# A graph network kernel: edge terms in two buffers, bias transfers inside the loop, and three groups of node rows loaded in the block before

## The chip, the cores and the metric

The kernel runs on one core of a Trainium2 chip. The metric is the device time of one execution in microseconds; the time before and after is the median of several runs. The kernel is written directly in Bass: each engine has its own instruction stream, and all ordering between engines is by semaphores that the author has placed.

## The reference, cut to what matters

```python
h = relu(layernorm(x))                                   # x: 50000 nodes x 128
x = x + leaky(( h + scatter(h[src]*ew/sqrt(deg..)) ) @ W0.T + b0)      # 12500 edges
h = relu(layernorm(x))
for l in range(4):                                       # graph attention, self loops added
    hw = h @ W[l]
    a  = leaky((hw @ a_s)[src] + (hw @ a_d)[dst] + (ea @ We[l]) @ a_e, 0.2)
    a  = segment_softmax(a, dst)
    h  = layernorm(segment_sum(hw[src] * a, dst) + b[l]) * g[l] + beta[l]
x = x + h
```

Most nodes have no edge. For those a layer is a fixed map of the node's own row, so all layers are done in one pass over the row ("dense"). Only the rows that edges touch go through the layers one at a time. `ea @ We[l]` meets only a fixed vector, so an edge needs just four numbers from its attributes, one for each layer: its edge terms.

## The kernel before, in words

The 50000 rows are 100 groups of 500 (125 partitions x 4 rows of 128 floats). The program is a chain of blocks; a block ends when all five engines have come to its end, and nothing of the next block starts earlier.

1. **Setup** (first block): weights, bias products, the scan columns of the edges. It ends with the four folded bias rows in `END[0:4]` (called `E4`).
2. **The setup loop** (second block, `with nc.Block()` after L636): 25 steps of 500 edges. SP loads the source numbers (L796) and target numbers (L177, L178 through `dma2`) of each step as a row that is broadcast to all partitions. DVE makes the masks and counts; PE turns the edge attributes and multiplies them by `VE` (L738) to a 4 x 500 tile of edge terms in PSUM; DVE copies that tile to the SBUF buffer `AES` (`keep_edge_term`, L683), and SP stores it to `term_t` (`place_edge_term`, L789). There is one `AES`: the copy of step g waits until the store of step g-1 has landed (`s_aet`). After the last step SP moves the bias rows of `E4` to the block matrix `EB`, 16 transfers of one row each (L813, L815), and waits for them. GpSimd (POOL) meanwhile gathers the first `SOON` = 44 of the 100 columns of source rows (L222); each gather is one indirect DMA of 125 rows, and it waits for nothing.
3. **The first dense block**: 36 groups. POOL runs the remaining gathers beside it, again without a wait.
4. **`conv_layer`**: the first layer of the touched rows.
5. Four times **a dense block of 16 groups and `attention(l)`**. In the dense block POOL gathers the rows of `row_t` that the preceding block has stored; it waits first for all those stores (`s_x1`, `s_rows`), then runs its 100 gathers, and the block cannot end before they have landed.

A dense block keeps 12 groups in a ring `X` in SBUF. At its start SP issues the loads of the first 12 groups, two DMAs each (112 and 13 partitions), and DVE's first `bn_stats` (L1051) waits for the first of them. The ring shares its memory with the masks `M` of `conv_layer` and `attention`: slots 0 to 2 lie where the mask of the first pairs lies. At the end of `conv_layer` and `attention` a side chain (END, XTX, a row of T) runs after the last pair of columns, step by step through PE, DVE and ACT, and SP stores its result last (L1348 and L1350, or L1823).

`wait_stores` makes SP wait at the start of such a block until all output rows of the dense block are written, before the masks are loaded over the ring.

Of the kernel before, what the change touches and what calls it, by code (L numbers as in the profile page):

```python
# [11 lines left out]
D = 128  # L12
N = 50000
E = 12500
L = 4
P = 125
C = E // P
# [14 lines left out]
SOON = 44  # L32


def gnn_kernel(nc, x, src, dst, ea, ew, w0, b0, wg, we, att_s, att_d, att_e, bg, gamma, beta, out):
    ctx = ExitStack()
    with ctx:
# [5 lines left out]
        def sem(name):  # L43
            return ctx.enter_context(nc.semaphore(name))
# [231 lines left out]
        VT = RB[0:C, 6700:6700 + D]  # L276
# [337 lines left out]
        s_aet = sem("edge_term_transposed")  # L614
# [19 lines left out]
        AES = AL[0:L, :, :].rearrange("l a e -> l (a e)")  # L634
        with nc.Block() as block:
# [7 lines left out]
            def _(dve):  # L643
# [35 lines left out]
                def keep_edge_term(g):  # L679
                    dve.wait_ge(s_aep, g + 1)  # L680
                    if g:
                        dve.wait_ge(s_aet, 16 * g)
                    nc.vector.tensor_copy(AES, PT[2 + g % 2][0:L, 0:Q * P]).then_inc(s_aes, 1)  # L683

# [93 lines left out]
            def _(sp):  # L778
                src_v = src_t.rearrange("t e -> (t e)")
                dst_v = dst_t.rearrange("t e -> (t e)")  # L780

                def keep_masks(k):
                    sp.wait_ge(s_mask, (k + 1) * EG // 5)
                    c0, c1 = k * C // 5, (k + 1) * C // 5
                    dma2(sp, m_v[:, c0:c1, :], M[:, c0:c1, :], s_mst)

                def place_edge_term(g):
                    sp.wait_ge(s_aes, g + 1)
                    sp.dma_start(term_t[:, g * Q * P:(g + 1) * Q * P], AES).then_inc(s_aet, 16)  # L789

                for g in range(EG):
                    if g >= 7:
                        place_edge_term(g - 7)
                    if g >= 3:
                        sp.wait_ge(s_ge, g - 2)
                    sp.dma_start(SRCB[g % 3], src_v[g * Q * P:(g + 1) * Q * P].unsqueeze(0)  # L796
                                 .broadcast_to([C, Q * P])).then_inc(src_rows[g % 3].s, 16)
                    if g >= 4:
                        sp.wait_ge(s_mask, g - 3)
                    dma2(sp, TGTB[g % 4], dst_v[g * Q * P:(g + 1) * Q * P].unsqueeze(0).broadcast_to([P, Q * P]),  # L800
                         dst_rows[g % 4].s)
                    if g > 5 and g % 5 == 3:
                        keep_masks(g // 5 - 1)
# [5 lines left out]
                sp.wait_ge(s_e4, 1)  # L809
                sp.wait_ge(s_ebz, 1)  # L810
                for a in range(Q):
                    for j in range(3):
                        sp.dma_start(EB[j * Q + a:j * Q + a + 1, a * D:(a + 1) * D],  # L813
                                     E4[j + 1:j + 2, :]).then_inc(s_eb, 16)
                    sp.dma_start(EB[KS - 1:KS, a * D:(a + 1) * D], E4[0:1, :]).then_inc(s_eb, 16)  # L815
                sp.wait_ge(s_eb, 16 * 4 * Q)
                sp.wait_ge(s_aet, 16 * EG)
# [10 lines left out]
        def dense(first_group, groups, moves, move, arrive, early=None):  # L828
# [39 lines left out]
            with nc.Block() as block:  # L868
# [11 lines left out]
                def _(sp):  # L880
                    for g in range(min(XS, groups)):
                        dma2(sp, rows(g), x_v[first_group + g], loaded[g % XS].s)
# [417 lines left out]

        def wait_stores(sp):
            for s in range(XS):
                sp.wait_ge(*signal(f"ring_stored_{s}").at(0))
# [16 lines left out]
        def conv_layer():  # L1320
# [13 lines left out]
            with nc.Block() as block:  # L1334
                @block.sync
                def _(sp):
                    wait_stores(sp)
                    load_masks(sp)
                    sp.dma_start(AE[:, :, :], term_t.rearrange("l (t e) -> t l e", t=C)).then_inc(s_aet, 16)
# [6 lines left out]
                    sp.wait_ge(s_aet, 16 * EG + 16)  # L1346
# [356 lines left out]
        def attention(l):  # L1703
# [100 lines left out]
            with nc.Block() as block:  # L1804
                @block.sync
                def _(sp):
# [10 lines left out]
                    else:  # L1817
                        for i in range(STORES):
                            c0, c1 = 2 * i * STORE, 2 * (i + 1) * STORE
                            sp.wait_ge(*t_ready.at((i + 1) * STORE))  # L1820
                            dma2(sp, row_v[:, c0:c1, :], T[:, c0:c1, :], s_rows)
                        sp.wait_ge(*x_act.at(1))
# [227 lines left out]
        for l in range(L):  # L2050
            targets = Targets(l)
            dense(done, SHARES[l + 1], C, refresh(l), [(s_refresh, 16 * C * (l + 1))], targets)
# [26 lines left out]
```

## Time and profile before

| | us |
|---|---|
| median of 3 runs | 2042.78 |
| the three runs | 2036.03, 2042.78, 2043.71 |
| the profiled execution | 2044.88 |
| its span in the trace | 2042.8 |
| mean granted clock of TensorE | 0.878 of full |

| stage | about from | to |
|---|---|---|
| setup | 0 | 48.7 |
| setup loop | 48.7 | 164.6 |
| dense, 36 groups | 164.6 | 510 |
| `conv_layer` | 510 | 763.7 |
| dense 0, attention 0 | 763.7 | 1064.8 |
| dense 1, attention 1 | 1064.8 | 1369.4 |
| dense 2, attention 2 | 1369.4 | 1673.9 |
| dense 3, attention 3 (final) | 1673.9 | 2042.8 |

A row of the timeline gives start, duration, engine, line, operation and, in brackets, the idle time ahead of it with what ended it. "SPq" rows are the moments at which SP issues a DMA, not the transfer itself. A row with "x3" merges several instructions.

### The profile page before, as it was taken

Reading aid. Unit: us, or ns where it says so; the run is one execution under the profiler, and the core shown is the slowest. Engines: PE = TensorE matmul, PEld = TensorE weight load, DVE = VectorE, ACT = ScalarE, POOL = GpSimd, SP = SyncE. Lnnn points to the kernel's source line nnn. Section 1 sums busy time; section 2 is a strip of 40 time slices with the busy share of each in tenths; the row PEclk is TensorE's granted clock in tenths of the full one; section 3 lists DMA queues with packets and bytes.
Section 4 is the critical chain, followed back from the end, with each engine's and each line's share of the span. In section 5 each row is a group of like instructions: output and inputs, shape, how many; then the busy total and the mean of one; then the engine's idle time right before and its main releaser. Section 6 shows DMA issues by size and latency. Waiting matters only on the chain. (4 is left out here: it accounts for less than half of the span.)

```text
span 2042.8 us, 40093 instructions
## 1 busy us (share of the span) xinstructions
PE 1536.4 (75%) x9041; PEld 1123.4 (55%) x9041; DVE 1630.1 (80%) x8491; ACT 1545.9 (76%) x7842; POOL 1089.7 (53%) x919
## 2 busy tenths in 40 slices
PE   3764888886788877885978884978875978875940
PEld 2433555553677764544975544975544975543830
DVE  5775999996899967986877986877986877986940
ACT  0674999996799967993987983988983978973730
POOL 0876787750455538772008771018771018772777
PEclk9996999998799977995997996988996988996975
DMA  8753233321321122213231213231213231214421
GB/s 165 194 145 91 73 100 97 97 72 37 92 67 55 55 71 65 60 41 85 66 101 39 61 45 79 68 109 33 61 41 90 67 107 25 61 45 119 110 53 34
DMA packets 134375, 157.14 MB, mean 77 GB/s; under 512 B 58714, under 2 KB 91879, under 8 KB 134137
## 3 DMA queue, kind: packets, MB, share of 16 engines
q1 hardware_dynamic: 77545, 128.36, 22.6%
q0 software_dynamic: 56160, 25.44, 6.0%
q8 instruction: 74, 1.21, 0.2%
q14 instruction: 164, 1.34, 0.2%
q10 hardware_dynamic: 432, 0.79, 0.1%
HBM read 106.25 MB, written 68.36 MB: 85 GB/s over the span
## 5 line engine op out<-in xcount | busy, mean ns | idle before, releaser
L222 POOL DMA_INDIRECT S<-row_t,rowI x400 | 537.9, 1345 | 562.0 <-DMA row_t<-T 422.4
L938 PE MATMUL bank<-AC,XT 128*125 128x390 f32 x800 | 327.9, 516 | 0.3
L1007 ACT ACTIVATE R<-bank 125x128 f32<-125x128 f32 x1200 | 322.8, 306 | 0.0
L1007 ACT ACTIVATION_READ_ACCUMULATOR R<-bank 125x1 f32 x1200 | 279.7, 240 | 0.0
L210 PE MATMUL bank<-ident,Y 125*128 125x125 f32 x800 | 131.2, 290 | 118.0 <-ACT Y L958 59.2
L1870 PE MATMUL bank<-WCX,XT 128*125 128x130 f32 (+1 forms) x1400 | 218.7, 279 | 0.1
L210 PEld LDWEIGHTS bank<-ident,Y 125*128 125x128 f32 x800 | 97.9, 150 | 218.3 <-issue 140.7
L222 POOL DMA_INDIRECT S<-in_x,srcI x100 | 157.9, 1579 | 99.7 <-issue 99.7
L1051 DVE BATCH_NORM_STATS2 st<-R 125x6 f32<-125x128 f32 x800 | 173.2, 279 | 31.0 <-issue 30.6
L1870 PEld LDWEIGHTS bank<-WCX,XT 128*125 128x125 f32 x1400 | 182.6, 189 | 6.7 <-ACT XT L1907 0.4
L918 PEld LDWEIGHTS bank<-AC,XT 128*125 128x125 f32 x800 | 105.6, 204 | 114.2 <-ACT SB L1024 112.6
L918 PE MATMUL bank<-AC,XT 128*125 128x128 f32 x800 | 124.7, 303 | 56.2 <-ACT SB L1024 55.0
L222 POOL DMA_INDIRECT T<-in_x,dstI x101 | 142.2, 1408 | 36.9 <-issue 36.9
L1849 PE MATMUL bank<-R,S 125*128 125x125 f32 x800 | 159.0, 281 | 2.9 <-DVE R L1955 1.9
L226 POOL DMA_INDIRECT out_rows<-T,repNI x101 | 123.4, 1221 | 70.6 <-DVE T L2012 39.4
L938 PEld LDWEIGHTS bank<-AC,XT 128*125 128x125 f32 x800 | 133.7, 197 | 44.5 <-ACT XT L991 8.6
L1851 PE MATMUL bank<-R,T 125*128 125x125 f32 x800 | 158.0, 280 | 0.0
L1029 ACT ACTIVATE R<-bank 125x128 f32<-125x128 f32 x400 | 108.5, 321 | 40.0 <-PE bank L922 39.1
L217 PE MATMUL bank<-W,R 128*125 128x128 f32 x800 | 128.8, 310 | 0.0
L1849 PEld LDWEIGHTS bank<-R,S 125*128 125x128 f32 x800 | 124.5, 196 | 3.6 <-DVE R L1955 2.1
L1897 ACT ACTIVATE R<-ident,aselfS 125x125 f32<-125x125 f32 x300 | 107.8, 431 | 23.2 <-PEq L1710 23.2
L1851 PEld LDWEIGHTS bank<-R,T 125*128 125x128 f32 x800 | 124.8, 197 | 0.0
(447 smaller groups left out, 4755.1 us busy)
## 6 DMA issues: line engine op xcount, KB each, us to landing
row_t<-T SPq DMA_DIRECT2D x40, 573.1 KB
R<-in_x SPq DMA_DIRECT2D x100, 224.0 KB
out_rows<-R SPq DMA_DIRECT2D x100, 224.0 KB
R<-m_t SPq DMA_DIRECT2D x25, 546.9 KB
S<-row_t,rowI POOLq DMA_INDIRECT x400
T<-in_edge_attr SPq DMA_DIRECT2D x5, 1120.0 KB
x_t<-XB SPq DMA_DIRECT2D x50, 112.0 KB
R<-x_t SPq DMA_DIRECT2D x25, 224.0 KB
```

What stands on the lines that cost most here:

```text
L210: ins = nc.tensor.transpose(ps[:, a * P:(a + 1) * P], t, ident[0:P, 0:P])
L217: ins = nc.tensor.matmul(pz[0:P, a, :], xt[:, a * P:(a + 1) * P], w, start=False, stop=True, skip_group_check=True)
L222: pool.indirect_dma_start(to, None, table, bass.IndirectOffsetOnAxis(ap=idx, axis=0), bounds_check=rows - 1, oob_is_err=False).then_inc(do ...
L226: pool.indirect_dma_start(table, bass.IndirectOffsetOnAxis(ap=idx, axis=0), frm, None, bounds_check=rows - 1, oob_is_err=False).then_inc(d ...
L918: nc.tensor.matmul(last_of(g)[:, a, :], h0(g, a), AC[3], start=a == 0, stop=False, skip_group_check=True)
L938: nc.tensor.matmul(LAYERS[a][0:P, 0:3 * D + 6], h0(g, a), ACB[:, 0:3 * D + 6], start=True, stop=True).then_inc(layers_done.s, 1)
L1007: ins = nc.scalar.activation(JUNK[:, a * 3 + l, :], LAYERS[a][0:P, l * D:(l + 1) * D], ACT.Square, scale=D ** -0.5, accum_out=NRM[:, g % N ...
L1029: ins = nc.scalar.activation(JUNK[:, 12 + a, :], last_of(g)[:, a, :], ACT.Square, scale=D ** -0.5, accum_out=ss4[:, g % NS, a:a + 1])
L1051: ins = nc.vector.bn_stats(ring[:, a, :], v[:, a, :])
L1849: nc.tensor.matmul(o, S[:, 2 * n + a, 0:D], MA[:, r, a, :], start=True, stop=False, skip_group_check=True)
L1851: ins = nc.tensor.matmul(o, T[:, 2 * n + a, 0:D], DGB[:, r, a, :], start=False, stop=True, skip_group_check=True)
L1870: ins = nc.tensor.matmul(product(banks[bank + r], 2 * P)[:, a, :], XT[:, r, xt + a * P:xt + (a + 1) * P], WCX[:, l, 0:cols], start=not fin ...
```

## The change

Three edits, and constants that go with them.

- **Edge terms in two buffers.** `AES` becomes a list of two: the old place in `AL` for even steps and columns 6300 to 6800 of `R` for odd ones. `s_aet` becomes two semaphores. The copy of step g now waits for the store of step g-2. The table `VT`, whose place the new buffer takes, moves to column 10900.
- **Bias transfers in the loop.** The 16 transfers of `E4` to `EB` leave the end of the block and go, one per step, into steps 2 to 17 of SP's loop (`place_bias`), behind the loads of that step.
- **`SOON` from 44 to 38.** POOL does 38 gathers in the setup loop and 62 of this kind in the first dense block.
- **Loads ahead.** The loads of groups 0 to 2 of each of the four dense blocks of 16 groups are issued by SP near the end of the block before (`load_ahead`), behind a wait that the last mask has been used (`masked.at(NU)`) and before the store of the side chain's result. The dense block's own load loop starts with group 3. The first dense block is left as it was.

```diff
-SOON = 44
+AHEAD = 3
+SOON = 38
...
-        VT = RB[0:C, 6700:6700 + D]
+        VT = RB[0:C, 10900:10900 + D]
...
-        s_aet = sem("edge_term_transposed")
+        s_aet = [sem("edge_term_placed_even"), sem("edge_term_placed_odd")]
...
-        AES = AL[0:L, :, :].rearrange("l a e -> l (a e)")
+        AES = [AL[0:L, :, :].rearrange("l a e -> l (a e)"), RB[0:L, 6300:6300 + Q * P]]
...
                 def keep_edge_term(g):
                     dve.wait_ge(s_aep, g + 1)
-                    if g:
-                        dve.wait_ge(s_aet, 16 * g)
-                    nc.vector.tensor_copy(AES, PT[2 + g % 2][0:L, 0:Q * P]).then_inc(s_aes, 1)
+                    if g >= 2:
+                        dve.wait_ge(s_aet[g % 2], 16 * (g // 2))
+                    nc.vector.tensor_copy(AES[g % 2], PT[2 + g % 2][0:L, 0:Q * P]).then_inc(s_aes, 1)
...
+                def place_bias(a, j):
+                    if a == 0 and j == 0:
+                        sp.wait_ge(s_e4, 1)
+                        sp.wait_ge(s_ebz, 1)
+                    k = j * Q + a if j < 3 else KS - 1
+                    sp.dma_start(EB[k:k + 1, a * D:(a + 1) * D], E4[(j + 1) % L:(j + 1) % L + 1, :]).then_inc(s_eb, 16)
...
                     dma2(sp, TGTB[g % 4], dst_v[g * Q * P:(g + 1) * Q * P].unsqueeze(0).broadcast_to([P, Q * P]),
                          dst_rows[g % 4].s)
+                    if 2 <= g < 18:
+                        place_bias((g - 2) // Q, (g - 2) % Q)
...
-                sp.wait_ge(s_e4, 1)
-                sp.wait_ge(s_ebz, 1)
-                for a in range(Q):
-                    for j in range(3):
-                        sp.dma_start(EB[j * Q + a:j * Q + a + 1, a * D:(a + 1) * D],
-                                     E4[j + 1:j + 2, :]).then_inc(s_eb, 16)
-                    sp.dma_start(EB[KS - 1:KS, a * D:(a + 1) * D], E4[0:1, :]).then_inc(s_eb, 16)
...
-                    for g in range(min(XS, groups)):
+                    for g in range(loaded_before, min(XS, groups)):
                         dma2(sp, rows(g), x_v[first_group + g], loaded[g % XS].s)
...
+        def load_ahead(sp, first_group):
+            for g in range(AHEAD):
+                dma2(sp, X[:, g * Q:(g + 1) * Q, :], x_v[first_group + g], signal(f"ring_loaded_{g}").s)
...
+                        sp.wait_ge(*masked.at(NU))
+                        load_ahead(sp, sum(SHARES[0:l + 2]))
                         sp.wait_ge(*x_act.at(1))
                         sp.dma_start(row_v[0:C, C, :], T[0:C, C, :]).then_inc(s_x1, 16)
```

SP's stream at the end of the setup loop, before (`EB<-END` is a bias transfer, `term_t<-AL` the store of an edge term, `R<-in_x` the next block's first load):

```order
L789 DMA term_t<-AL 4x500 x4
L177 DMA m_t<-R 112x2500
L178 DMA m_t<-R 13x2500
L789 DMA term_t<-AL 4x500 x3
L813 DMA EB<-END 1x16x8 x3
L815 DMA EB<-END 1x16x8
```

The same place now:

```order
L797 DMA term_t<-R 4x500
L178 DMA m_t<-R 112x2500
L179 DMA m_t<-R 13x2500
L797 DMA term_t<-AL 4x500
L797 DMA term_t<-R 4x500
L797 DMA term_t<-AL 4x500
L636 UNCONDITIONAL_BRANCH
```

The 16 transfers that stood behind the last edge term are gone from the end; each now stands behind the target loads of one step, and the stores alternate between the two buffers.

SP's stream at the end of attention 0, before (`row_t<-T 100x131` is the store of the side chain's result):

```order
L177 DMA row_t<-T 112x1310
L178 DMA row_t<-T 13x1310
L1823 DMA row_t<-T 100x131
L1804 UNCONDITIONAL_BRANCH
L879 UNCONDITIONAL_BRANCH
L177 DMA R<-in_x 112x512
L178 DMA R<-in_x 13x512
```

The same place now:

```order
L178 DMA row_t<-T 112x1310
L179 DMA row_t<-T 13x1310
L178 DMA R<-in_x 112x512
L179 DMA R<-in_x 13x512
L178 DMA R<-in_x 112x512
L179 DMA R<-in_x 13x512
L178 DMA R<-in_x 112x512
L179 DMA R<-in_x 13x512
L1835 DMA row_t<-T 100x131
L1814 UNCONDITIONAL_BRANCH
L883 UNCONDITIONAL_BRANCH
```

Six load issues now stand between the last large row store and the small one. At the end of `conv_layer` they stand before the two stores of the side chain in the same way.

## Rows read from the trace of the kernel before

**Rows 1.** The page, busy time of each engine (share of the span) and instructions.
```profile
PE 1536.4 (75%) x9041; PEld 1123.4 (55%) x9041; DVE 1630.1 (80%) x8491; ACT 1545.9 (76%) x7842; POOL 1089.7 (53%) x919
```

**Rows 2.** Busy time of each engine from 150 to 200 us, then clock, DMA share, GB/s.
```profile
150.00:200.00 50.00, 20.65 (x80) 13.35 (x80) 27.65 (x167) 21.45 (x94) 28.12 (x22) 0.63 0.36 89
```

**Rows 3.** Timeline of SP's DMA issues at the end of the setup loop.
```profile
150.50 2.39 SPq L789 DMA_DIRECT2D term_t<-AL  x2
153.00 1.85 SPq L813 DMA_DIRECT2D EB<-END  x3
...
164.63 0.34 SPq L177 DMA_DIRECT2D R<-in_x  x1
```

**Rows 4.** The group of DVE's edge-term copies, and the last one in the timeline.
```profile
L683 DVE COPY AL<-bank 4x500 f32<-4x500 f32 x25 | 16.6, 663 | 18.8 <-DMA term_t<-AL 18.8
...
151.95 0.67 DVE L683 COPY AL<-bank 4x500 f32<-4x500 f32 x1 [1.48 <-DMA term_t<-AL]
```

**Rows 5.** Waits of SP's queue: total us, times, longest.
```profile
SPq L789 <- DVE AL L683: 40.4, 22, 3.2
```

**Rows 6.** Busy time in two stretches of the loop, as in rows 2.
```profile
56.00:66.00 10.00, 9.61 (x46) 5.93 (x44) 8.16 (x18) 7.42 (x24) 8.31 (x6) 1.00 0.84 195
...
106.00:116.00 10.00, 6.29 (x40) 4.10 (x40) 7.08 (x16) 8.51 (x33) 8.78 (x5) 1.00 0.75 203
```

**Rows 7.** Timeline of POOL: the first, the 38th and the 44th gather of the loop.
```profile
49.69 1.43 POOL L222 DMA_INDIRECT S<-in_x,srcI  x1 [46.11 <-issue]
...
132.22 1.27 POOL L222 DMA_INDIRECT S<-in_x,srcI  x1 [0.30 <-issue]
...
146.51 1.27 POOL L222 DMA_INDIRECT S<-in_x,srcI  x1 [0.30 <-issue]
```

**Rows 8.** The page's group of `bn_stats`, and timelines at the heads of dense blocks.
```profile
L1051 DVE BATCH_NORM_STATS2 st<-R 125x6 f32<-125x128 f32 x800 | 173.2, 279 | 31.0 <-issue 30.6
...
167.64 0.29 DVE L1051 BATCH_NORM_STATS2 st<-R 125x6 f32<-125x128 f32 x1 [15.02 <-issue]
...
763.71 0.32 SPq L177 DMA_DIRECT2D R<-in_x  x1
...
766.60 0.29 DVE L1051 BATCH_NORM_STATS2 st<-R 125x6 f32<-125x128 f32 x1 [3.65 <-issue]
...
1064.78 0.32 SPq L177 DMA_DIRECT2D R<-in_x  x1
...
1064.79 1.28 ACT L973 ACT_TABLE_LOAD   x1 [0.80 <-PEq L1804]
...
1067.51 0.29 DVE L1051 BATCH_NORM_STATS2 st<-R 125x6 f32<-125x128 f32 x1 [3.96 <-issue]
```

**Rows 9.** End of attention 0: DMA traffic in one microsecond, the side store, POOL's first gather.
```profile
1062.00:1063.00 1.00, 0.59 (x4) 0.37 (x3) 0.26 (x1) 0.00 (x0) 0.00 (x0) 1.00 0.98 299
...
1064.02 0.27 SPq L1823 DMA_DIRECT2D row_t<-T  x1
...
1066.50 1.27 POOL L222 DMA_INDIRECT S<-row_t,rowI  x1 [130.59 <-DMA row_t<-T]
```

**Rows 10.** Last gather and DVE's last work of dense 0 and 3; POOL's last of all.
```profile
934.58 1.33 POOL L222 DMA_INDIRECT S<-row_t,rowI  x1 [0.30 <-issue]
...
938.86 0.69 DVE L1207 TENSOR_TENSOR R<-R 125x512 f32<-125x512 f32 x1
...
1843.59 1.58 POOL L222 DMA_INDIRECT S<-row_t,rowI  x1 [0.30 <-issue]
...
1849.76 0.69 DVE L1207 TENSOR_TENSOR R<-R 125x512 f32<-125x512 f32 x1
...
2037.96 1.19 POOL L226 DMA_INDIRECT out_rows<-T,repNI  x1 [0.30 <-issue]
```

**Rows 11.** SP's slowest DMA issue, in the first block.
```profile
35.01 5.78 SPq L178 DMA_DIRECT2D T<-in_edge_attr  x1
```

More of the change, by code:

```diff
@@ L788, in place_edge_term @@
                     sp.wait_ge(s_aes, g + 1)
-                    sp.dma_start(term_t[:, g * Q * P:(g + 1) * Q * P], AES).then_inc(s_aet, 16)
+                    sp.dma_start(term_t[:, g * Q * P:(g + 1) * Q * P], AES[g % 2]).then_inc(s_aet[g % 2], 16)
                 for g in range(EG):
@@ L808, in _ @@
                     place_edge_term(g)
-                sp.wait_ge(s_e4, 1)
-                sp.wait_ge(s_ebz, 1)
-                for a in range(Q):
-                    for j in range(3):
-                        sp.dma_start(EB[j * Q + a:j * Q + a + 1, a * D:(a + 1) * D],
-                                     E4[j + 1:j + 2, :]).then_inc(s_eb, 16)
-                    sp.dma_start(EB[KS - 1:KS, a * D:(a + 1) * D], E4[0:1, :]).then_inc(s_eb, 16)
                 sp.wait_ge(s_eb, 16 * 4 * Q)
-                sp.wait_ge(s_aet, 16 * EG)
+                sp.wait_ge(s_aet[0], 16 * (EG - EG // 2))
+                sp.wait_ge(s_aet[1], 16 * (EG // 2))
                 sp.wait_ge(s_mst, 160)
@@ L826, in gnn_kernel, with dense @@
             k.base += 32
-        def dense(first_group, groups, moves, move, arrive, early=None):
+        def dense(first_group, groups, moves, move, arrive, early=None, loaded_before=0):
             loaded = [signal(f"ring_loaded_{s}") for s in range(XS)]
@@ L1338, in _ @@
                     load_masks(sp)
-                    sp.dma_start(AE[:, :, :], term_t.rearrange("l (t e) -> t l e", t=C)).then_inc(s_aet, 16)
+                    sp.dma_start(AE[:, :, :], term_t.rearrange("l (t e) -> t l e", t=C)).then_inc(s_aet[0], 16)
                     for n in range(NU):
@@ L1345, in _ @@
                             dma2(sp, row_v[:, 2 * (n + 1 - STORE):2 * n + 2, :], T[:, 2 * (n + 1 - STORE):2 * n + 2, :], s_rows)
-                    sp.wait_ge(s_aet, 16 * EG + 16)
+                    sp.wait_ge(s_aet[0], 16 * (EG - EG // 2) + 16)
+                    sp.wait_ge(*masked.at(NU))
+                    load_ahead(sp, SHARES[0])
                     sp.wait_ge(*x_stage.at(10))
@@ L1821, in _ @@
                             dma2(sp, row_v[:, c0:c1, :], T[:, c0:c1, :], s_rows)
+                        sp.wait_ge(*masked.at(NU))
+                        load_ahead(sp, sum(SHARES[0:l + 2]))
                         sp.wait_ge(*x_act.at(1))
@@ L2051, in gnn_kernel @@
             targets = Targets(l)
-            dense(done, SHARES[l + 1], C, refresh(l), [(s_refresh, 16 * C * (l + 1))], targets)
+            dense(done, SHARES[l + 1], C, refresh(l), [(s_refresh, 16 * C * (l + 1))], targets, AHEAD)
             targets.end()
```

## The prediction, made before the changed kernel was run

> **What bounds the kernel now.** I read the page first. DVE is busy for 80% of the span and ACT for 76% [rows 1]; no engine is full over the whole, so the time that can be won lies in stages where both are idle together. The table of stages shows such a stretch between 150 and 200 us, where PE has 20.65, DVE 27.65 and ACT 21.45 us of work in 50 [rows 2]. The timelines around it say why. DVE's last edge-term copy starts at 151.95 [rows 4], the last store of terms is issued by 152.9, and then SP issues one bias transfer after another from 153.00 on; the next block's first load is issued only at 164.63 [rows 3]. All engines stand at the block's end for that time, and SP alone sets it.
>
> Inside the loop DVE is nearly the bound, but it idles 18.8 us in front of its 25 copies, all of it until a term store has landed [rows 4]. That is a ring: copy, issue, landing, next copy.
>
> Third, the heads of the dense blocks. The group of `bn_stats` has 31.0 us of idle time before it, 30.6 of it "issue" [rows 8], and five waits make it up: 15.02 at the first dense block (which includes the bias tail), 3.65 and 3.96 at the next two, so 8.0 for the last two together, 4.0 each. In the second of these SP issues the load at 1064.78 and DVE starts at 1067.51; ACT, which needs no load, starts at 1064.79.
>
> **The bias transfers.** From the last term store to the next block is now 152.65 (the second of the two issues at 150.50; the merged row ends at 152.89) to 164.63, 12.0 us. Without the 16 transfers SP waits only for that store. The store issued at 150.50 released the copy at 151.95, so landing takes 1.45 us, and a change of block takes 0.5 (SP's 1064.02 + 0.27 to 1064.78 in rows 8 and 9). That leaves 2.0 us: **10.0 us gained**. The price in the loop: one transfer per step, at up to 0.62 us of SP (1.85 for three), 10 us in all. SP waits 40.4 us in the loop for the copies alone [rows 5], so this fits. Behind each stands the next term store and the next loads, which are asked for two to three steps ahead; the waits for `E4` and the cleared `EB` were met one block earlier and cost nothing.
>
> **Two buffers.** The 18.8 us of DVE's idle time can go at most, since a store then has two steps to land. What comes next is DVE itself or the DMA engines. The 25 steps run from about 56 to 152.6, 3.9 us each; 18.8 / 25 = 0.75 of it is this idle time, so DVE's own floor is about 3.1. They are busy for 0.75 of the time at 203 GB/s in one stretch and 0.84 at 195 in another [rows 6]. The loop's bytes stay the same while it shrinks by a fifth, so the share must rise from about 0.7 towards 0.85, and landings get slower behind the mask stores. I take 15.6 of the 18.8, about a sixth off for that. Ends: 18.8 if nothing else comes late, 0 if the loop is held by its transfers anyway. The idle time of DVE names landings only and never a source or target row, so I choose near the upper end.
>
> The Trainium skill, in "DMA: Bandwidth & Descriptors", section "Why a DMA increments its semaphore by 16 and not by 1", says that a transfer of 100 partitions is spread over 10 of the 16 DMA engines only. The source rows have 100 partitions. By that rule the mean share of 0.75 hides ten fuller engines, and the loop would gain perhaps half as much; no view here splits the share by engine, so it only adds to the chance of the second rival.
>
> **`SOON`.** POOL's 38th gather starts at 132.22 and ends at 133.5, the 44th ends at 147.8 [rows 7]. The loop should now end near 152.65 - 15.6 = 137.1, plus 2.0 for landing and block: the next block starts at about 139. With 44 gathers POOL would have held the block until 148; with 38 it has some 5 us to spare. The six gathers that move run in the first dense block, beside ACT and DVE at work; six times the gather's 1.6 us there is 10 us, and POOL's stream in that block ends long before the block does. I cost it at nothing; if that cover were gone it would be those 10 us.
>
> **Loads ahead.** DVE could start about 0.1 us after SP's first issue in the block: 766.60 - 763.81 = 2.8 us, 1067.51 - 1064.88 = 2.6, and the last two like the second (idle 4.0 against 3.96), 10.7 together. ACT's table load of 1.28 us [rows 8] ends at 1066.07; ACT needs it after DVE's statistics, 1.3 us after the new start, 1066.2, so it just stays hidden.
>
> Two things can take some of it back. First, the six load issues, 2.4 us of SP, stand before the side store. At attention 0 the last large row store has been issued by 1061.3 and the side store goes at 1064.02 [rows 9], so they fit with 0.3 us to spare. But their 750 KB stand before the small store in the DMA engines: at 299 GB/s [rows 9] 2.5 us of traffic, of which about 1.7 is still ahead of it. POOL's first gather, now at 1066.50, may start up to 1.7 us later. The first group itself stands behind 640 KB of rows; that traffic is over at about 1063.4 and 250 KB take 0.84 us, so it lands just in time. At `conv_layer` SP has no work between 754.5 and 760.8 and nothing is delayed.
>
> Second, POOL's 100 gathers may end a dense block last. In dense 0 the last gather ends at 935.91 and DVE at 939.55, SP's stores 0.8 later; in dense 3 it is 1845.17 and 1850.45 [rows 10]. DVE moves up by 2.8 and 2.65, POOL does not, or goes back by 1.7 in dense 3. What is left, with the 0.8, is 1.6 and 1.7 us for the last gather to land. That landing isn't shown alone: from POOL's last instruction at 2039.15 to the span's end at 2042.8 are 3.65 us, which bounds it from above, and the edge-term store's 1.45 is the nearest row below. I take 1.7, between them and near the lower one because the upper holds the end of the program too. So dense 0 and 3 sit at the edge; at 3.65 each would lose 2 us. In dense 1 and 2 POOL's last gather ends over 7 us before DVE, and nothing is lost. I take off 1.0 in all: **9.7 us gained**, with 6 and 10.7 as ends.
>
> **The sum.** 10.0 + 15.6 + 9.7 = 35.3 us. Against the profiled execution, 2044.88 (span 2042.8, 2.1 outside it), that is 2009.6. The median of the runs is 2.1 lower, 2042.78, which gives 2007.5; I say **2008**. A measurement tells about 0.5%, 10 us, from no change.
>
> **Rivals.**
>
> *DMA holds the loop* (0.13). The share goes to its limit and the landings move back with it. For it: 0.84 at only 195 GB/s in rows 6. Against: other stretches move 299 GB/s. Then the two buffers bring 0 to 8 of the 15.6: 2015 to 2023.
>
> *POOL ends the setup loop last* (0.10). Its gathers take 2.23 us each on average here, against 1.6 alone. If they slow down in proportion to the DMA share, 0.7 to 0.84, it is 2.7 each, and 38 of them end at 152: 13 us are lost, 2021. For it: gathers in the loop are already slow. Against: they are delayed by a fixed number of bytes, which doesn't grow. The Trainium skill, "DMA: Bandwidth & Descriptors", section "Queues, rings and completion order", has each DMA engine take turns between the queues it has work for, packet by packet. By that a denser SP queue costs each gather more; it is what this rival would rest on.
>
> *The heads give little* (0.09). POOL's chain, not DVE's, ends the dense blocks, or the first group isn't there: 2 to 5 us instead of 9.7, 2012 to 2016.
>
> *The change does not do what it says* (0.04), because the block's end is held by something that no row names: within 5 us of before, 2040.
>
> *Slower* (0.02). SP issues can stall: one took 5.78 us behind five large loads [rows 11]. If each of the six loads ahead took over about 2.5 us, the side store would be 13 us late in four blocks, of which 2 to 5 are slack: 4 x 9 = 36 us, which eats the whole gain; at the full 5.78 it is 2090. It decides at 2.5 us per issue; the same loads now take 0.4.
>
> **How the numbers follow.** The forecast itself has 0.62. Its own range, from the ends of the parts, is 2000 (18.8 and 10.7 in full, and a run as low as the fastest of before) to 2014. To hold 8 in 10 I reach to most of the next two rivals: 1999 to 2020. Faster by over 0.5%: 0.94; the same 0.04; slower 0.02.
>
> **What would show it.** In the changed kernel's trace: SP's first load of the first dense block at 139, not before 136 nor after 146; DVE's copies with under 4 us of idle time; no bias transfers behind the last term store; POOL's 38th gather over by 137; the idle time of `bn_stats` down from 30.6 to about 9 us, with heads of about 1.2; POOL's first gather in dense 1 to 3 up to 1.7 us further behind the block's start; the last landing and DVE's end within 1 us of each other in dense 0 and 3. If the copies' idle time is gone but source, target or gather rows show new waits, the rival on DMA is right; if the heads shrink and the dense blocks' lengths from their start grow by as much, POOL's chain ended them.

## The result

The changed kernel takes **2013.8 us** (median of four runs, 2012.8 to 2016.1) against 2041.8 for the kernel before: a ratio of 0.9869, 95% interval 0.9847 to 0.9891. The forecast was 2008 with a range of 1999 to 2020. The profiled execution has a span of 2010.8 us, 32.0 less than before. All that follows about places is read from it. In the changed code L683 has become L684, L789 L797, L177 and L178 L178 and L179, L222 L223, L1051 L1055 and L1823 L1835.

```profile
PE 1526.6 (76%) x9041; PEld 1114.3 (55%) x9041; DVE 1629.9 (81%) x8491; ACT 1546.6 (77%) x7842; POOL 1089.0 (54%) x919
...
L1055 DVE BATCH_NORM_STATS2 st<-R 125x6 f32<-125x128 f32 x800 | 172.9, 277 | 16.1 <-issue 8.9
```

The busy times are those of [rows 1] within 10 us; what went is idle time. That before `bn_stats` fell from 31.0 [rows 8] to 16.1.

Where it went shows when one lists SP's first load of each block that starts with loads. The convolution's length is in the second line.

| block starts at | before | after | gained so far | gained in the stage |
|---|---|---|---|---|
| first dense block | 164.63 | 140.09 | 24.5 | setup 24.5 |
| dense 0, behind the convolution | 763.71 | 734.80 | 28.9 | 4.4 |
| dense 1 | 1064.78 | 1034.77 | 30.0 | 1.1 |
| dense 2 | 1369.36 | 1337.93 | 31.4 | 1.4 |
| dense 3 | 1673.88 | 1641.35 | 32.5 | 1.1 |
| end of the span | 2042.8 | 2010.8 | 32.0 | -0.5 |

The setup gave 24.5 where 25.6 was forecast, the heads of dense 0 to 3 gave 3.1 instead of 9.7, and 4.4 came in a stage to which the forecast gave nothing. Within the setup the two terms came out otherwise than forecast: the last copy ends 18.2 us earlier (152.62 to 134.44) where 15.6 was forecast, and from there to the next block it is 5.65 us instead of 12.0, a gain of 6.4 where 10.0 was forecast.

**The end of the setup loop.** First the groups of DVE's copies by shape, which answer [rows 4], then SP's waits in the loop, as [rows 5], then the timelines of SP and POOL, which answer [rows 3] and [rows 7]:

```profile
L684 DVE COPY AL<-bank 4x500 f32<-4x500 f32 x13 | 8.6, 659 | 1.3 <-DMA term_t<-AL 1.2
L684 DVE COPY R<-bank 4x500 f32<-4x500 f32 x12 | 7.9, 659 | 2.4 <-DMA term_t<-R 2.4
```
```profile
SPq L797 <- DVE R L684: 9.9, 6, 3.4
SPq L797 <- DVE AL L684: 6.9, 8, 2.6
SPq L636 <- PEq L636: 3.7, 1, 3.7
```
```profile
133.88 0.24 SPq L797 DMA_DIRECT2D term_t<-R  x1
134.46 0.24 SPq L797 DMA_DIRECT2D term_t<-AL  x1
140.09 0.33 SPq L178 DMA_DIRECT2D R<-in_x  x1
```
```profile
133.23 1.27 POOL L223 DMA_INDIRECT S<-in_x,srcI  x1 [0.30 <-issue]
134.81 1.27 POOL L223 DMA_INDIRECT S<-in_x,srcI  x1 [0.30 <-issue]
140.95 1.27 POOL L223 DMA_INDIRECT S<-in_x,srcI  x1 [4.87 <-issue]
```

DVE idles 3.7 us before its copies instead of 18.8, and no bias transfer stands behind the last term store. But that store's issue starts at 134.46 and the next block comes 5.6 us later, where the forecast had 2.0; SP stands 3.7 us of it at the block's end with its own work done. The last thing running is POOL's 38th gather, which ends at 136.08, 4.0 us before the block. The windows show the hole (busy time of PE, PEld, DVE, ACT and POOL, then clock, DMA share and GB/s, as in [rows 2]): everything but POOL has next to nothing to do there.

```profile
125.00:135.00 10.00, 6.43 (x35) 3.35 (x33) 9.01 (x18) 7.76 (x29) 8.48 (x6) 0.98 0.33 94
135.00:145.00 10.00, 0.00 (x0) 0.00 (x0) 1.26 (x11) 0.30 (x1) 4.52 (x4) 0.50 0.42 108
```

**A head.** The timeline at the start of dense 1, answering [rows 8] and [rows 9]:

```profile
1032.77 0.31 ACT L1951 ACTIVATE YX<-T 100x128 f32<-100x128 f32 x1 [2.46 <-DVE T L2041]
1032.98 0.19 ACT L1951 ACTIVATION_READ_ACCUMULATOR YX<-T 100x1 f32 x1
...
1033.49 0.39 SPq L179 DMA_DIRECT2D R<-in_x  x1
1033.93 0.33 SPq L1835 DMA_DIRECT2D row_t<-T  x1
1034.77 0.32 SPq L178 DMA_DIRECT2D R<-in_x  x1
...
1034.86 0.29 DVE L1055 BATCH_NORM_STATS2 st<-R 125x6 f32<-125x128 f32 x1 [2.12 <-PEq L1814]
...
1037.91 1.27 POOL L223 DMA_INDIRECT S<-row_t,rowI  x1 [133.18 <-DMA row_t<-T]
```

DVE starts 0.1 us behind SP, as forecast (0.1 at dense 0 and 2 too, 0.5 at dense 3); before it was 2.7. But the side store (L1835) waits for the last of the six load issues: ACT is done at 1033.17 and the store goes at 1033.93, 0.76 us later. And POOL's first gather comes 3.14 us behind the block's start; it was 1.72.

**An end.** The timeline at the end of dense 2. `m_t` is the next block's first load, normally issued 1.7 us behind the end of the last output store:

```profile
1509.78 1.27 POOL L223 DMA_INDIRECT S<-row_t,rowI  x1 [0.30 <-issue]
...
1511.56 0.32 SPq L178 DMA_DIRECT2D out_rows<-R  x1
1511.92 0.39 SPq L179 DMA_DIRECT2D out_rows<-R  x1
...
1515.11 0.32 SPq L178 DMA_DIRECT2D R<-m_t  x1
```

Here it comes 2.8 us behind that store and 4.1 us behind the last gather's end (1511.05). Dense 3 is alike, 3.3 and 4.5 us. Against the usual 1.7 that is 1.1 and 1.6 us lost.

### The profile page after: what moved, and what is told of

The parts are those of the page before. It is cut to its first block and busy times, and to the rows that moved or that the text cites. A ratio compares the mean times of both kernels' runs of the same rounds, so it can differ in the third digit from the quotient of the medians.

```text
span 2010.8 us, 40093 instructions
## 1 busy us (share of the span) xinstructions
PE 1526.6 (76%) x9041; PEld 1114.3 (55%) x9041; DVE 1629.9 (81%) x8491; ACT 1546.6 (77%) x7842; POOL 1089.0 (54%) x919
## 5 line engine op out<-in xcount | busy, mean ns | idle before, releaser
L223 POOL DMA_INDIRECT S<-row_t,rowI x400 | 537.8, 1344 | 560.8 <-DMA row_t<-T 420.7
L223 POOL DMA_INDIRECT S<-in_x,srcI x100 | 158.3, 1583 | 83.6 <-issue 83.6
L1055 DVE BATCH_NORM_STATS2 st<-R 125x6 f32<-125x128 f32 x800 | 172.9, 277 | 16.1 <-issue 8.9
L227 POOL DMA_INDIRECT out_rows<-T,repNI x101 | 124.2, 1230 | 68.0 <-issue 34.7
L223 POOL DMA_INDIRECT T<-in_x,dstI x101 | 140.4, 1390 | 37.4 <-issue 37.4
```

The lines of the kernel that those rows point to most:

```text
L223: pool.indirect_dma_start(to, None, table, bass.IndirectOffsetOnAxis(ap=idx, axis=0), bounds_check=rows - 1, oob_is_err=False).then_inc(do ...
L227: pool.indirect_dma_start(table, bass.IndirectOffsetOnAxis(ap=idx, axis=0), frm, None, bounds_check=rows - 1, oob_is_err=False).then_inc(d ...
L1055: ins = nc.vector.bn_stats(ring[:, a, :], v[:, a, :])
```

## The experiments

Three questions were open: what holds the end of the setup loop, where the heads' gain went, and whether the 4.4 us belong to the change. Places are read from the profile of each run, and all differences in a total are taken from its ratio to the kernel before.

**1. Fewer and more gathers in the setup loop.**

```diff
-SOON = 38
+SOON = 30
```


> The changed kernel with SOON at 30 instead of 38: eight gathers fewer in the setup loop, eight more in the first dense block. In the changed kernel the last term store is issued at 134.5 and POOL's 38th gather ends at 136.1, but the next block's first load comes only at 140.1. Theory (POOL holds the block, about 3.5 us behind its last gather): POOL is through long before, the block ends by SP's last landing, and the first load of the first dense block comes at 134.7 + 1.45 + 0.5 = 136.7; 3.4 us are gained there. Rival 1 (the last term store lands late, after about 4.9 us): the first load stays at 140. Rival 2 (POOL's eight gathers more lengthen the first dense block): the first load comes at 136.7, but the block's length from there grows by up to 8 x 1.6 = 13 us. Total by the theory 2010, by rival 1 2014, by rival 2 up to 2023.

```diff
-SOON = 38
+SOON = 44
```


> The changed kernel with SOON at 44, as in the kernel before. Six gathers more in the setup loop, at 1.6 us alone: the last one starts near 134.8 + 9.5 = 144.3 and ends at 145.6, or 3 us later if POOL makes one of its pauses (about one in 39 gathers) on the way. Theory (about 3.5 us from the last gather's end to the block's end, whatever the gather's number): the next block's first load comes 4.0 us behind the last gather's end, at 149.6 to 152.6. Rival (the 4.0 us at the 38th gather were the pause that POOL makes every 39 gathers): the pause now stands in front of the 39th or 40th gather, and the first load comes 0.5 to 1 us behind the last gather's end. Total 2024 by the theory, some 3 us less by the rival; about 2014 if POOL didn't hold the block at all.

SP and POOL at the end of the loop with 30:

```profile
132.60 0.24 SPq L797 DMA_DIRECT2D term_t<-AL  x1
134.44 0.33 SPq L178 DMA_DIRECT2D R<-in_x  x1
...
135.29 1.27 POOL L223 DMA_INDIRECT S<-in_x,srcI  x1 [13.57 <-issue]
```

and with 44:

```profile
142.06 1.28 POOL L223 DMA_INDIRECT S<-in_x,srcI  x1 [3.17 <-issue]
...
148.38 1.27 POOL L223 DMA_INDIRECT S<-in_x,srcI  x1 [0.30 <-issue]
...
152.24 0.33 SPq L178 DMA_DIRECT2D R<-in_x  x1
```

With 30 gathers the block follows 1.8 us behind the start of the last term store's issue (1.6 behind its end): a little less than the forecast's 2.0, and 5.65 us earlier than with 38. So POOL held the block, and the store's landing didn't. The total is 2006.8 (0.9839, interval 0.9814 to 0.9864); its interval overlaps that of 38, so it is the block's start that shows this and not the total. The eight gathers that moved cost nothing behind it: the first dense block and the convolution take 594.6 us, with 38 they take 594.7. With 44 the last gather ends at 149.65 and the block comes 2.6 us behind it; the total is 2022.9 (0.9904). The price is there behind another gather too, but smaller: neither the 4.0 of the theory nor the 0.5 to 1 of the rival. The pause does stand where the rival put it, before the 40th gather (the row at 142.06).

**2. Is it the gather, or POOL?** `SOON` 30, `AHEAD` 1, and POOL kept at work on something that moves no data:

```diff
-AHEAD = 3
-SOON = 38
+AHEAD = 1
+SOON = 30
...
                 gather_x(pool, S, srcI, 0, SOON, s_xsrc)
+                for k in range(60):
+                    nc.gpsimd.memset(RB[0:C, 11040:11168], 0.0).then_inc(s_fill, 1)
+                    pool.wait_ge(s_fill, k + 1)
```


> SOON at 30 and AHEAD at 1, and behind POOL's 30 gathers of the setup loop 60 chained memsets of 100 x 128 into an unused place (0.19 us each elsewhere, near 0.25 with the chain, so that POOL works on until 136 to 142, as with 38 gathers). Only the kind of POOL's last instruction differs from the changed kernel. Theory (the 4.0 us between the last gather's end and the next block belong to the gather, whose transfer isn't over when its instruction is): the next block's first load comes 0.5 to 1 us behind the last memset's end. Rival (any last instruction of POOL costs the block that long): 4.0 us behind it.

POOL's and SP's timelines (L644 and L801 are the memset and the store of terms in this kernel):

```profile
116.62 2.54 POOL L223 DMA_INDIRECT S<-in_x,srcI  x1 [0.30 <-issue]
119.17 17.17 POOL L644 MEMSET R<- 100x128 f32 x60
140.16 1.28 POOL L223 DMA_INDIRECT S<-in_x,srcI  x1 [3.83 <-issue]
```
```profile
133.29 0.24 SPq L801 DMA_DIRECT2D term_t<-AL  x1
139.29 0.33 SPq L178 DMA_DIRECT2D R<-in_x  x1
```

My theory falls (the total, 2007.4, is one execution). The last gather was over at 119.2, the last memset at 136.34, and the block comes 2.95 us behind that, not 0.5 to 1. So of the 4.0 us most isn't the gather's: a block that POOL ends last costs about 3 us from POOL's last instruction, for both kinds tried, where one that SP ends costs 0.5. What adds the fourth microsecond behind the 38th gather and not behind the 44th stays open. The Trainium skill, "Perfetto Trace Analysis", section "GPSIMD Engine Instruction", says to take spans of this engine in a profile as unreliable; that may blur the gathers' ends, but the chained memsets' row has ends that the semaphores tie down to 0.3 us each.

**3. The parts alone**, each put into the kernel before. First the bias transfers:

```diff
                     dma2(sp, TGTB[g % 4], ...)
+                    if 2 <= g < 18:
+                        place_bias((g - 2) // Q, (g - 2) % Q)
...
-                for a in range(Q):
-                    for j in range(3):
-                        sp.dma_start(EB[...], E4[j + 1:j + 2, :]).then_inc(s_eb, 16)
-                    sp.dma_start(EB[KS - 1:KS, ...], E4[0:1, :]).then_inc(s_eb, 16)
```


> The kernel before with the 16 bias transfers in the loop, one in each of 16 steps, and nothing else. Theory (the forecast's first term): the loop keeps its length, the last term store is issued by 152.9, and the first load of the first dense block comes at 154.6 instead of 164.63: 10.0 us gained, 2031.8. Rival 1: with one term buffer each transfer's issue delays the next store and so the next copy; up to 0.62 x 16 = 9.9 us come back in the loop, which ends at up to 162.5, 2041. Rival 2: POOL's 44th gather, which ended at 147.8, plus 4.0 us, 151.8: doesn't hold. If the loads wait for the bias transfers in the DMA queue, DVE's idle time before the copies rises above 18.8 us.

The last term stores and the next block, and the group of copies:

```profile
150.74 4.69 SPq L796 DMA_DIRECT2D term_t<-AL  x3
157.02 0.33 SPq L177 DMA_DIRECT2D R<-in_x  x1
```
```profile
L683 DVE COPY AL<-bank 4x500 f32<-4x500 f32 x25 | 16.6, 662 | 19.8 <-DMA term_t<-AL 15.8 <-issue 4.0
```

The total is 2031.9 (0.9950, interval 0.9934 to 0.9967: 10.2 us, 6.7 to 13.5), the forecast's 10.0. In the trace the block starts 7.6 us earlier: the tail is gone in full (155.43 to 157.02), and the loop ends 2.5 us later, with 4.0 us of idle time before the copies that no landing explains. So a part of the first rival is there in the one-buffer loop, a quarter of its 9.9 us.

Then the two buffers alone (the second `AES`, its semaphores and `VT` moved; bias transfers behind the loop, `SOON` 44):

> The kernel before with the two term buffers and nothing else (the bias transfers behind the loop, SOON at 44, no loads ahead). Theory: DVE's idle time before the copies falls from 18.8 to under 4 us and the last term store is issued near 134; the bias transfers take it to 145, and then POOL's 44th gather, ending near 149.7, plus 2.6 us holds the block's end: first load of the first dense block at 152.3, 12.3 us gained, 2029. Rival (POOL doesn't hold it): 134.5 + 12 = 146.6, 18 us gained, 2024. By the forecast's term alone, 15.6, it is 2026.

2027.9 (0.9927, interval 0.9900 to 0.9954: 15 us, 9 to 20). In its trace the copies idle 0.3 and 2.2 us, the last bias transfer is issued by 144.3, POOL's 44th gather ends at 149.20, and the block starts at 151.86, 2.66 behind it. The rival, 146.6, is out: without the change of `SOON` POOL eats 6 us of what the buffers bring (144.3 + 1.6 against 151.86). That is what the line with 38 is for, and 38 isn't few enough.

**4. The loads ahead.** Without them, and alone in the kernel before:

```diff
-AHEAD = 3
+AHEAD = 0
```


> The changed kernel with AHEAD at 0: the setup as changed, no loads ahead. The forecast's third term said that these bring 9.7 us, which gives 2013.8 + 9.7 = 2023.5. New theory, from the two traces: only about 3 us of it are there (32.0 gained over the whole span less 28.9 gained up to the first dense block behind the convolution), because the side store is 0.8 us later in three blocks, POOL's last gather holds two block ends, and in the first of these dense blocks a second stretch of the low PE clock, 35 to 42 us behind its start, takes the head's gain back: 2017. In this kernel's trace that second stretch should then be missing from the first of those blocks, as in the kernel before.

> The kernel before with the loads ahead (three groups) and nothing else. By the forecast's third term 2042 - 9.7 = 2032. New theory: 3 us, 2039, within what a measurement can tell from no change; the setup part as before (first load at 164.6), the side store of dense 1 to 3 issued 0.75 us behind ACT's end, the low clock again 35 to 42 us behind the start of the first dense block behind the convolution.

And with one group instead of three:

```diff
-AHEAD = 3
+AHEAD = 1
```


> The changed kernel with AHEAD at 1: one group of rows (two loads) is loaded at the end of the preceding block instead of three (six loads). In the changed kernel the side store of the attention blocks is issued 0.75 to 0.8 us behind the end of ACT's work on it, since SP is still issuing loads, and the first gather of dense 1 to 3 starts 3.1 to 3.6 us behind the block's start instead of 1.7. Theory: the side store goes out 0.1 us behind ACT again, so that dense 1 to 3 each start 0.7 earlier; DVE still starts with the block; the gathers start 1.9 to 2.2 us behind the block's start (250 KB instead of 750 ahead of the store), and dense 2 and 3, which POOL's last gather ends, end 1.2 us earlier beyond that: in all 3 x 0.7 + 2 x 1.2 = 4.5 us, 2009. Rival 1: the second group, now issued at the block's start, isn't there for DVE's second step, each dense block loses 1 us, 2013 to 2014 or no change. Rival 2: the store waits behind large row stores and not behind these loads, so the gathers start at 3.1 still, 2012.

The loads alone bring 4.3 us (2038.7; ratio 0.9979, interval 0.9967 to 0.9990: 2.0 to 6.7). 9.7 is outside. The setup alone gives 2021.7 (0.9889), between the two expectations, with an interval of 11 us that holds both; and its expected mark was missed, since a second stretch of low clock stands in dense 0 there too. With one group: 2009.5 (0.9847, interval 0.9829 to 0.9865), as expected. Its timeline at the start of dense 1:

```profile
1033.62 0.19 ACT L1951 ACTIVATION_READ_ACCUMULATOR YX<-T 100x1 f32 x1
1033.83 0.28 SPq L1835 DMA_DIRECT2D row_t<-T  x1
1034.63 0.32 SPq L178 DMA_DIRECT2D R<-in_x  x1
...
1035.33 0.29 DVE L1055 BATCH_NORM_STATS2 st<-R 125x6 f32<-125x128 f32 x1 [1.96 <-PEq L1814]
...
1036.43 1.27 POOL L223 DMA_INDIRECT S<-row_t,rowI  x1 [131.02 <-DMA row_t<-T]
```

The side store goes 0.02 us behind ACT, and POOL's first gather 1.80 behind the block's start. DVE starts 0.7 us behind SP here; its group's first load was issued at 1031.18, 4.15 us before, so this may be the landing.

The lengths of the dense blocks, from their first load to the next block's first load, in the traces (us; four executions each, of kernels whose dense blocks are alike but for the loads ahead; those with `AHEAD` 1 include experiments 2 and 5):

| | dense 0 | dense 1 | dense 2 | dense 3 | sum of means |
|---|---|---|---|---|---|
| none (before, bias alone, setup alone, buffers alone) | 178.3 178.4 180.9 179.1 | 180.6 180.5 179.4 179.7 | 180.4 179.3 179.6 179.3 | 179.4 179.8 179.6 179.5 | 718.5 |
| three groups (after, `SOON` 30, `SOON` 44, loads alone) | 177.7 177.7 177.7 177.6 | 178.0 178.1 178.2 178.6 | 177.2 178.2 178.1 177.2 | 178.0 179.3 178.4 179.4 | 712.3 |
| one group (`AHEAD` 1; with `SOON` 30, 34 and the memsets) | 177.8 178.0 177.7 177.7 | 178.6 176.4 175.9 178.7 | 177.1 176.1 176.2 176.1 | 177.2 176.2 176.2 176.2 | 708.0 |

With one group the blocks are 10.5 us shorter than with none, the forecast's 10.7. With three they are 6.2 shorter, and three side stores are 0.75 late: 3.9 is left, which agrees with the 4.3 of the loads alone.

**5. Both settings together.**

```diff
-AHEAD = 3
-SOON = 38
+AHEAD = 1
+SOON = 30
```


> The changed kernel with SOON at 30 and AHEAD at 1 together. Theory (the two costs are independent: POOL at the setup loop's end, and six load issues ahead of the side store): 5.6 us from the first (block start 134.4 instead of 140.1) and 3 to 4.5 from the second, 2013.8 - 9 = 2005 or a little less. Rival: where the low clock falls in a dense block moves with each small shift and takes 2 to 3 us back or gives them: 2002 to 2009.

2003.6 us (0.9806, interval 0.9782 to 0.9830), better than the change as it was made by 10 us after the medians and by 13 after the ratios; 9 were expected. In its trace the block starts at 136.33 and not at 134.4, 1.6 us behind the issue of a last term store that came later here (134.50). Four gathers moved back in don't matter:

> SOON at 34 and AHEAD at 1. POOL's 34th gather should end near 129.5; 4.0 us later is 133.5, before SP's last term store has landed (about 136). Theory: the block's end is SP's, as with 30, the first load comes at 134.5 to 136.5, 2003.5 in all, no change from 30 that can be measured; if gathers moved out of the setup loop cost something later, it is up to 4 x 1.6 us less here, 1997. Rival: the gathers slow the loop's own stores, and the first load comes 1 us later than with 30.

2004.5 (0.9810). The block starts at 136.06, 1.6 us behind the last term store (134.23 + 0.24).

**6. The clock.** In dense 0 the loads ahead won 2.8 us at the head, and the first output store came only 0.3 us earlier in the block (57.5 us behind its start instead of 57.7). The windows of 5 us show why; PEclk is the third number from the end, 1.00 being TensorE's 2.4 GHz and 0.50 its 1.2. The kernel before, 25 to 40 us into dense 0:

```profile
788.71:793.71 5.00, 4.15 (x15) 2.43 (x14) 3.33 (x21) 4.03 (x20) 4.09 (x4) 0.72 0.07 11
793.71:798.71 5.00, 3.96 (x20) 2.33 (x18) 4.56 (x24) 5.00 (x31) 4.08 (x4) 1.00 0.10 15
798.71:803.71 5.00, 3.36 (x19) 2.31 (x20) 3.80 (x36) 4.39 (x30) 4.09 (x4) 1.00 0.06 10
```

and the changed kernel at the same place, 5 us further:

```profile
759.80:764.80 5.00, 3.95 (x20) 2.64 (x21) 3.36 (x27) 4.39 (x26) 4.09 (x4) 1.00 0.09 13
764.80:769.80 5.00, 2.31 (x13) 1.53 (x12) 3.90 (x27) 4.39 (x23) 4.08 (x4) 0.97 0.09 15
769.80:774.80 5.00, 5.00 (x15) 2.87 (x14) 3.23 (x20) 3.61 (x23) 3.96 (x4) 0.50 0.07 10
774.80:779.80 5.00, 4.87 (x23) 3.26 (x22) 3.32 (x23) 4.24 (x25) 3.90 (x4) 0.85 0.08 11
```

The clock rises earlier than before (0.72 in the first window of before, 1.00 here). But behind a stretch in which PE has only 2.31 us of work (it idles 2.69 us in one piece before 768.63), it falls again for about 7 us, at first with PE busy without a pause. The kernel before has the same idle piece, and a stretch with as little work, and keeps its clock there:

```profile
800.35 0.62 PE L210 MATMUL bank<-ident,Y 125*128 125x125 f32 x4 [2.68 <-ACT XT L991]
...
795.52:800.52 5.00, 2.32 (x14) 1.51 (x13) 4.88 (x34) 4.87 (x25) 4.09 (x4) 1.00 0.08 13
```

So the idle piece alone does not bring the fall. All eight executions with loads ahead and no added matmuls have the fall at this place (weakest with `SOON` 34, 0.72 in one window), and two of the four without (setup alone and buffers alone), so the loads are not its only cause. These two took 180.9 and 179.1 us in dense 0, the two without the fall (before and bias alone) 178.3 and 178.4. In the kernel before dense 1 to 3 have such a fall and dense 0 has none. The Trainium skill, "TensorE: Matmul & The Clock Gate", section "HAM oscillation — how this bites in real kernels", says that waits between bursts of matmuls bring the clock down again each time. The changed kernel's rows agree, those of the kernel before do not: the same wait leaves the clock at 1.00 there. To test the idle time as a cause, it was filled in every dense block, with `SOON` 30 and `AHEAD` 1:

```diff
+                    def keep_busy(g):
+                        if g == 0:
+                            for _ in range(12):
+                                nc.tensor.matmul(banks[4][0:P, 0:116], W0[:, 0:P], W0[:, 0:116], start=True,
+                                                 stop=True, skip_group_check=True)
...
-  (5, add_biases), (0, turn1),
+  (5, add_biases), (4, keep_busy), (0, turn1),
```


> SOON at 30 and AHEAD at 1, and in every dense block 12 matmuls of 128x116 whose result nobody reads, put into TensorE's idle time (2.7 us in the first dense block behind the convolution) in front of the fifth group's first transposes. Theory (the second stretch of the low clock in that block, 35 to 42 us behind its start, is what takes the head's gain back): with that time filled the granted clock stays at 1.00 from 24 us on, the block's length from its start to the next block's first load falls from 178.0 to about 175.7, the other three stay within 0.7 of 176.4, 176.1 and 176.2. Total 2001. Rival (the clock falls anyway, or the matmuls themselves delay the transposes by 1 to 2 us in five blocks): 178 or more, total 2004 to 2010.

The same four windows:

```profile
757.95:762.95 5.00, 3.84 (x21) 2.53 (x20) 3.37 (x27) 4.39 (x27) 4.09 (x4) 1.00 0.08 13
762.95:767.95 5.00, 4.92 (x37) 4.17 (x36) 4.10 (x29) 4.38 (x22) 4.09 (x4) 1.00 0.09 15
767.95:772.95 5.00, 4.73 (x26) 2.93 (x25) 4.09 (x23) 5.00 (x28) 4.09 (x4) 1.00 0.07 10
772.95:777.95 5.00, 4.67 (x22) 2.54 (x21) 3.58 (x32) 5.00 (x36) 3.94 (x4) 1.00 0.09 14
```

The clock stays up and dense 0 takes 175.74 us instead of 178.0, as expected to a tenth. This is one execution, against eight of eight that fell at this place without the matmuls. Dense 1 and 3 take 176.0; dense 2 has its low stretch one group earlier, out of reach of these matmuls, and takes 178.2. Without the matmuls dense 2 had the same low stretch (0.57 and 0.75 at 25 to 35 us, against 0.60 and 0.71 here) and took 176.1, so the stretch does not explain these 2 us; their cause is open. A last run filled that place as well (9 more, there alone):

> As with the 12 unread matmuls per dense block, and in the third dense block behind the convolution alone 9 more, one group earlier, in front of the fourth group's first transposes, where TensorE idles for 2.1 us and the granted clock then falls to 0.60 (25 to 30 us behind the block's start). Theory: that second low stretch goes too; the block's length from its start to the next block's first load falls from 178.2 to near 176.0, the other blocks stay as they are (175.7, 176.0 and 176.0), and the whole is 2 us faster, 2000 to 2001. Rival (which blocks have a second low stretch changes from one execution to the next, and the matmuls have nothing to do with it): the length stays at 178 in this block, or low stretches appear in others.

Dense 2 takes 174.9 with the clock at 1.00 from 20 us on. But in the same execution dense 0, whose code is that of the run before it, got its clock 5 us earlier, lost it at 25 to 35 us, and took 176.5. And dense 1 and 3, which have none of the nine, kept their clock at 1.00 as well, one of them across an idle piece of 2.07 us. So that the nine matmuls kept it up in dense 2 isn't shown. What is shown is that without the idle piece dense 0 did not lose its clock in the execution with the 12, and that the piece is there in blocks that lose it and in blocks that don't. That the moment at which the clock rose makes the difference fits these rows, but no run varied it; the rival holds for that half. The totals, 2002.4 (0.9797) and 2002.5 (0.9805, interval 0.9792 to 0.9818), can't be told from 2003.6.

## Why the prediction was right, and where its steps weren't

- **Bias tail, 10.0.** Right within its interval: 10.2 measured alone, 6.7 to 13.5. The loop's price, put at nothing, is 2.5 us in the trace with one buffer, so that the block starts 7.6 us earlier there. With two buffers DVE's idle time shows none of it.
- **Two buffers, 15.6 of 18.8.** Right: DVE's idle time fell by 15.1, and the last copy ends at 134.44 instead of 152.62, 18.2 us. The last term store is issued between 132.6 and 135.8 in the ten kernels with this loop and `SOON` of 30 to 44, so the 2.6 us more than forecast aren't a finding. The rival of the DMA engines is out: 3.7 us of idle time is left. With it goes the estimate by the Trainium skill's page "DMA: Bandwidth & Descriptors", section "Why a DMA increments its semaphore by 16 and not by 1", on ten of 16 engines for 100 partitions: nothing of the loop's gain was lost.
- **`SOON`, "some 5 us to spare".** This step failed. The gather did end by 137, as forecast (136.08), yet it held the block: I charged nothing between POOL's last instruction and the block's end, and it is 4.0. The price is 3.6 us here (140.1 instead of the 136.5 that the forecast's 2.0 gives behind this store). The row for it was in hand, 3.65 us behind POOL's last instruction [rows 10], and I had read it as the program's end. The rival "POOL ends the setup loop last" is thus half true: POOL does end it, by its exit and not by slower gathers.
- **Loads ahead, 9.7.** This step failed too; 4.3 was measured. DVE's heads were right (0.1 us behind SP in three of four), and with one group the 10.7 are there. The sign for them was missed all the same: `bn_stats` idles 16.1 us where about 9 was forecast, 8.9 in front of the first dense block, which is the POOL step above, and 2.1 to 2.5 in front of dense 1 to 3, where 1.2 was forecast. What was mis-sized is what three groups cost. The six issues do not fit "with 0.3 us to spare" before the side store: they need 3.34 us (1030.54 to 1033.88), as the first one takes 1.23 us behind the row stores, not 0.4. The side store is late by 0.75 in each of three blocks for that. The store's landing moved POOL's first gather by 1.4, 1.4 and 1.9 us, near the 1.7 forecast. And the end of a dense block by POOL, 4.1 to 4.7 us from its last gather to the next block's load where I had 2.2, holds dense 2 and 3 instead of 0 and 3, for 1.1 and 1.6 us. How much of the 4.1 to 4.7 is the last gather's landing and how much POOL's exit isn't shown. The late stores and the two ends make 4.9 of the 5.4 us that are missing.
- **Dense 0.** Its head was right and its end isn't POOL's (904.74 against DVE's 909.99). The clock took the gain. That two executions with equal code in a block differ by 2 us for this, the forecast didn't have.
- **4.4 us in the first dense block and the convolution.** No run ties it to the change. That stretch lasts from 594.6 to 600.8 us in the fourteen traces; the kernel before (599.1) and the changed one (594.7) lie at either side. The three shortest are kernels with three groups ahead (594.6, 594.7, 595.4), but the fourth of these, with the loads alone, took 600.3, so an order by edit isn't shown.
- **A slip in the rival "Slower".** Its own steps give 2044 at 2.5 us per issue, but about 2120 and not 2090 at 5.78 (six issues, 34.7 us, less the 2.7 they fit into and some 4 of slack, in four blocks). No issue among the loads ahead took over 1.23, so nothing hangs on it.

The measured time is 5.8 us above the forecast, at the upper edge of its own range of 2000 to 2014. The two steps that failed account for 3.6 and 5.4, both of the same sign and together more than the 5.8. That the time came out nearer is luck: the loop ended 2.6 us earlier than forecast, which its idle time (15.1 us for 15.6) doesn't account for, and the rest is within what the intervals leave open. The profiled execution hides most of the miss, as its 4.4 us in the first stage point the other way. For the loads ahead it is the rival "the heads give little", which I gave 0.09, that came true: it had 2 to 5 us for them and 2012 to 2016 in all, and 4.3 and 2013.8 were measured. Its mechanism, POOL at the dense blocks' ends, is one of three that took the gain, beside the late side stores and the clock in dense 0.

## What to carry to other kernels

Charge an engine's exit from a block as well as its last instruction: here SP's cost 0.5 us and POOL's about 3, so POOL's work in a block must end 3 to 4 us before the others'. Of the loads moved ahead into a block's end only the first group paid here; each further issue stands before whatever small store the next block waits for. A gain at the head of a block isn't a gain at its end where the clock is still low: look at the granted clock over the whole first part of the block, in more than one execution.

## What the runs showed of the hardware that I had not expected

- Leaving a block costs 1.6 us from the last small store's issue (its landing included) when SP is last, and 2.6 to 4.0 us from POOL's last instruction in the setup loop when POOL is, even 17 us behind its last gather (2.95).
- POOL's stream of gathers has pauses, most of 2.4 to 3.9 us and the longest 6.1: one before the 40th gather of the setup loop where it has 44 (3.17 in the row above at 142.06), in the dense blocks behind the convolution one before the 40th and one before the 79th of the 100. They have no releaser in the trace. A block's change restarts the count: with `SOON` 30, 34, 38 and 44 the first pause in the first dense block stands before gather 70, 74, 78 and 84, the 40th of that block each time.
- The large part of a group's load (112 partitions, 229 KB) took SP 1.2 us to issue right behind the two parts of a row store, in each of the four blocks, and 0.35 otherwise (1.23 at 1030.54 in the changed kernel, 0.35 for the next).
- TensorE's granted clock went from 1.00 to 0.50 behind a stretch of 5 us with 2.31 us of work and one idle piece of 2.69; filled with unread matmuls, it stayed at 1.00. The same idle piece (2.68) left it at 1.00 in dense 0 of the kernel before. In the one pair where only this differs the fall cost the block about 2.3 us (178.0 and 175.74).
